# A scan and routed-experts layer on one core: the last weight set loaded behind the first row lists, and the second block's low part and turns moved

## What is computed

```python
xn = _layernorm(x, axis=-1)
x = x + _L0_attn_ref(xn, ...) + _L0_ffn_ref(xn, ...)
# attn: g, v, d = xn @ Wg + bg, xn @ Wv + bv, xn @ Wd + bd
#       h[t] = (0.001 + 0.998 * sigmoid(d)) * h[t-1] + sigmoid(g) * tanh(v)
# ffn:  scores = sigmoid(xf @ Wg.T + bg + bias); the two highest of 8 per token
#       out = gelu(xf @ Ws1.T + bs1) @ Ws2.T + bs2
#           + sum over the two of score * (gelu(xf @ W1[e].T + b1[e]) @ W2[e].T + b2[e])
```

## Time and profile before

| | us |
|---|---|
| median of 3 runs | 669.68 (669.53 to 670.26) |
| the profiled execution | 669.86 |
| its span, first to last instruction | 668.1 |
| PE busy | 640.3 (96%) |
| DVE busy | 535.2 (80%) |
| ACT busy | 407.1 (61%) |
| POOL busy | 277.1 (41%) |

### The profile page before, as it was taken

One profiled execution on the slowest core, in us unless ns is written; L12 is line 12 of the kernel. 1 busy time (PEld: TensorE's weight loads), 2 busy tenths in 40 slices (PEclk: granted clock), 3 DMA queues, 4 the chain that ended last, 5 costly groups with the idle time before them and its releaser, 6 DMA issues.

```text
span 668.1 us, 19052 instructions
## 1 busy us (share of the span) xinstructions
PE 640.3 (96%) x6168; PEld 506.0 (76%) x6168; DVE 535.2 (80%) x1431; ACT 407.1 (61%) x701; POOL 277.1 (41%) x262
## 2 busy tenths in 40 slices
PE   7989999999999998699999999999999999999994
PEld 6565756566665756588889988898889889898983
DVE  6988998999999889488887777677777767777774
ACT  6849696969687874264745454555555555555552
POOL 3043241324242541354545444435445555555423
PEclk9999999999999999799999999999999999999998
DMA  7324526171625242352424253545657576666732
GB/s 259 132 33 128 150 74 189 65 191 36 186 42 180 65 127 64 98 151 45 71 52 80 48 132 106 131 106 141 173 126 200 128 195 184 144 177 179 197 57 28
DMA packets 69472, 81.29 MB, mean 122 GB/s; under 512 B 25684, under 2 KB 61460, under 8 KB 66568
## 3 DMA queue, kind: packets, MB, share of 16 engines
q1 hardware_dynamic: 54264, 62.35, 30.8%
q0 software_dynamic: 15120, 17.77, 15.4%
HBM read 38.66 MB, written 18.10 MB: 85 GB/s over the span
## 4 chain that ended last, share of the span: by engine, by line
PE 80%; DVE 10%; issue 6%; ACT 2%; DMA 1%; another core or an unknown queue 0%; POOLq 0%; POOL 0%; DVEq 0%; ACTq 0%
PE bank L1340 31%; PE bank L1332 29%; PE bank L1320 6%; PE bank L1368 5%; PE bank L1391 4%; PE bank L1410 2%; DVE arena L953 2%; DVE arena L952 2%; DVE W L833 1%; PE bank L1311 1%; PE bank L1275 1%; DMA arena<-in_x 1%; DVE small L842 1%; ACT arena L644 1%; ACT W L612 1%
## 5 line engine op out<-in xcount | busy, mean ns | idle before, releaser
L1340 PE MATMUL bank<-W,arena 128*128 (+1 forms) x2112 | 278.5, 274 | 4.0 <-DVE arena L953 3.3
L1332 PE MATMUL bank<-rows,W 128*128 128x256 f16 (+1 forms) x1728 | 273.8, 296 | 3.4 <-issue 1.8
L655 ACT ACTIVATE arena<-bank,par 128x256 f32<-128x256 f32 (+2 forms) x344 | 166.8, 517 | 142.2 <-PE bank L1332 116.0
L1340 PEld LDWEIGHTS bank<-W,arena 128*128 128x128 f16 x2112 | 202.4, 98 | 40.6 <-issue 6.3
L1332 PEld LDWEIGHTS bank<-rows,W 128*128 (+1 forms) x1728 | 165.3, 98 | 57.2 <-issue 5.8
L576 POOL DMA_INDIRECT out<-arena,slot_adds x71 | 117.7, 1657 | 136.3 <-DVE arena L1217 71.8
L952 DVE TENSOR_SCALAR arena<-arena,par 128x256 f16<-128x256 f32 (+1 forms) x284 | 99.8, 351 | 55.8 <-ACT arena L655 36.5
L953 DVE SCALAR_TENSOR_TENSOR arena<-arena,par 128x256 f16<-128x256 f32 (+1 forms) x284 | 134.0, 472 | 10.1
L516 POOL DMA_INDIRECT lists<-entry,place x64 | 67.9, 1061 | 108.4 <-ACT arena L637 63.3
L1320 PE MATMUL bank<-rows,W 128*128 128x512 f16 x288 | 63.9, 379 | 0.1
L661 ACT ACTIVATE rows<-bank 128x1024 f16<-128x1024 f16 (+2 forms) x43 | 36.1, 839 | 43.8 <-PE bank L1410 31.1
(11 more groups left out here) (190 smaller groups left out, 546.3 us busy)
## 6 DMA issues: line engine op xcount, KB each, us to landing
stage<-in_w SPq DMA_DIRECT2D x36, 512.0 KB, 4.0
stage<-W SPq DMA_DIRECT2D x14, 1024.0 KB, 5.2
arena<-W SPq DMA_DIRECT2D x8, 1024.0 KB, 5.6
arena<-in_x SPq DMA_DIRECT2D x8, 512.0 KB
xhl_rows<-W SPq DMA_DIRECT2D x8, 512.0 KB
out<-arena SPq DMA_DIRECT2D x8, 512.0 KB
b2row<-in_b SPq DMA_DIRECT2D x22, 128.0 KB
arena<-in_b SPq DMA_DIRECT2D x21, 128.0 KB
```

The costliest lines, as they stand in the source:

```text
L655: ins = A(h32[k][:, c], ps_e[k][:, c], ACT.Gelu, bias=p[:, 4 + e * i + jj:5 + e * i + jj], scale=p[:, 0:1])
L1332: ins = T.matmul(bank_, weights(w, wp * HALF + c * H + j * P, P), rhs[:, 2 * xp + c, :], start=n == 0, stop=n == 3 * KD - 1)
L1340: ins = T.matmul(banks[t // 2][:, (t % 2) * D:(t % 2 + 1) * D], h[:, hp, t * P:(t + 1) * P], weights(w, (2 + wp) * HALF + j * D, D), start ...
```

## The change

Three things are moved; no instruction is added or removed, apart from where it stands.

1. SP: the four loads of set 8 leave the end of the loop over b and the end of slot 0's pass, and stand together behind the row list of slot 4, ahead of the values of slot 2.
2. End of sequence 0: DVE makes the second x's low part behind `split_wide(0, 5)`, the sixth split, instead of behind the eighth. PE turns high and low part one after the other behind the seventh `layer2`; before, the first turn stood there and the second behind the eighth.
3. Slots 4 to 7: DVE's `bias_rows` stands behind the seventh split instead of the sixth.

```diff
@@ SP, loop over b
-                if b:
+                if 0 < b < SEQS - 1:
                     for part in range(2):
                         next_weights(b + 1, 0, part)
@@ SP, loop over the slots
                 if n + 4 < SLOTS:
                     rows_list(s, order(n + 4))
+                if n == 0:
+                    for l in range(2):
+                        for part in range(2):
+                            next_weights(NW - 1, l, part)
                 if n + 2 < SLOTS:
                     values_of(s, order(n + 2))
...
                     adds_list(s, order(n + 2))
-                if n == 0:
-                    for part in range(2):
-                        next_weights(NW - 1, 1, part)
@@ DVE, opening
                 split_wide(0, 5)
+                x_low(1)
                 residual(0, 0, 1)
                 split_wide(0, 6)
                 split_wide(0, 7)
-                x_low(1)
                 low_turned(1, 1)
@@ DVE, slot
-                    if j == 5:
+                    if j == (6 if low is not None else 5):
                         bias_rows(s)
@@ PE, sequence
-                    if first and i >= 6:
-                        pe.wait_ge(*((xhi_ok, 2), (xhl_ok, 2))[i - 6])
-                        pe.wait_ge(*((r_ok, 2), (ev_act, RING + EVENTS))[i - 6])
-                        x_transposes(1, i - 6, (ps_t16, ps_low16[1])[i - 6])
+                    if first and i == 6:
+                        pe.wait_ge(xhl_ok, 2)
+                        pe.wait_ge(r_ok, 2)
+                        x_transposes(1, 0)
+                        pe.wait_ge(ev_act, RING + EVENTS)
+                        x_transposes(1, 1, ps_low16[1])
```

## The result

| | us |
|---|---|
| before, median of 4 runs | 669.66 (669.53 to 670.26) |
| changed kernel, median of 4 runs | 660.51 (660.00 to 661.39) |
| ratio | 0.9863, 95% interval 0.9846 to 0.9880 |
| its profiled execution, and the span | 661.39, 659.6 |

The change saves 9.15 us, 1.4%. That is less than the 1.4 us between the lowest and the highest of the four runs. The gain forecast against the medians, 8.2 us, lies inside the interval of the ratio (8.0 to 10.3 us), and between the two profiled executions the gain was 669.86 - 661.39 = 8.47, where 8.25 was forecast. So the question for the runs is where the other 0.7 to 0.9 us of the medians come from.

A forecast was written before the change was run, and what follows sets the result against it. PE was taken to set the pace, with its main hole at the hand-over to the slots. From 669.86, less 7.8 and 0.45, came 661.6, or 661.4 against the median; forecast 661.5, range 660.6 to 664.0 us.

The forecast's parts named there:

- Where the time lies: Hand-over from sequence 7 to slot 0: PE idles 6.27 us because SP waits to issue set 8's loads before the lists.
- The next thing late: Hand-over: with the gather's wait gone, DVE's eighth split, ending at 267.40, holds the last `layer2`.
- Size of part 1: Hand-over: moving the loads starts slot 0's second layer 7.8 us earlier, bounds 7.5 and 7.85.
- slack: Hand-over: gathered rows are there at about 264.2, PE wants them at 266.55, leaving 2.3 us.
- Part 2: End of sequence 0: moving low part and turns starts the logits earlier, gaining 0.45 us, bounds 0.3 and 0.5.
- the sum of PE's work: End of sequence 0: PE's gapless work from the seventh `layer2`, 43.87 to 47.55, takes 3.68 us in either order.
- the low part costs 0.33: End of sequence 0: the earlier low part delays later splits, so the seventh `layer2` starts at 44.2 instead of 43.87.
- Part 3: Slots 4 to 7: moving the bias rows costs 0, from 0.2 us gained to 0.3 lost.
- Loads behind the lists: Slots 0 and 1: the four loads, 2 MB, issued from 272.0 ahead of slot 2's values, cost nothing.
- The cover claimed: Slot 1: 10.5 us from the loads' issue to squaring the first part at 282.5, against landings of 4.2 to 7.3.
- The recorded estimate of 7.4 us: Slots 0 and 1: transfer time for 2.5 MB of loads and store at the skill's 341 GB/s.
- The range: Whole kernel: 660.6 to 664.0 us at 8 in 10, from term bounds 7.8 to 8.35, 0.4 scatter and most of one rival.

The follow-up runs named there:

- part 1 alone: Only the four loads of set 8 moved, against the kernel before: 656.12 against 663.88 us, ratio 0.9884.
- e7_one_ahead: Changed kernel with the first of the four loads left ahead of the row lists: 662.21 us against 664.10 for the kernel before, ratio 0.9969.
- e9_low_only: Kernel before with only DVE's low part moved behind the sixth split, PE's turns unmoved: 670.78 against 670.63 us, ratio 0.9997.
- e3_bias: Kernel before with only the bias rows of slots 4 to 7 moved: 664.12 us, ratio 1.0003.
- e6_no_bias: Changed kernel without the bias rows' move: 655.38 us against 664.10 for the kernel before, ratio 0.9871.
- e4_all: The whole changed kernel again, against the kernel before: 655.53 against 663.88 us, ratio 0.9872.
- e8_loads_late: Changed kernel with the four loads put behind slot 6's row list: 661.43 us against 664.10 for the kernel before, ratio 0.9956.
- e12_before_again: Kernel before, unchanged, traced again on the slower kind of chip: 669.95 us.
- e11_all_again: The whole changed kernel a third time, against the kernel before: 661.73 against 670.63 us, ratio 0.9867.
- e10_turns_only: Kernel before with only PE's turns moved behind the seventh `layer2`, low part unmoved: 670.41 against 670.63 us, ratio 1.0001.
- e5_before: Kernel before, unchanged, traced again on the faster kind of chip: 663.63 us.

## Why the prediction was off by a little: right in its mechanisms, short in its terms

**Where the time lies: right.** The hole at the hand-over was SP's queue, and it went away with part 1 alone (7.7 of 8.4 us). The next thing late was the eighth split, as named, and PE's wait for it 0.45 us.

**Size of part 1: the term that was mis-sized. It fits the execution that was read and is short for the median.** 7.85 was worked out and 7.8 taken; the two profiled executions give 7.76. But the hand-over of before was read from one execution, 14.11 us, and seven traces give 13.55 to 14.90 with a mean of 14.36. The kernels without a load ahead give 6.32 to 6.35. The mean gain is therefore 8.0, and single executions lie between 7.2 and 8.6. On the slower kind of chip, that of the comparison, the four traces have a mean of 14.53, so a gain of 8.2; on the faster kind three have 14.14, so 7.8. The forecast's bounds for this term, 7.5 to 7.85, described how DVE or PE would continue behind the hole and left out that the hole itself has a length that varies, with the landing of a small list behind big loads. The row for this was there (3.36 us for the list, a transfer of 2 KB) and was taken as a constant; without the loads it is 2.5. In the changed kernel that made no difference to PE, since there was slack (2.3 us by the forecast, 3.5 measured in e7_one_ahead), but it was the sign that the 14.38 us of POOL's wait held a DMA whose duration varies: 3.13 to 4.42 us with the two loads ahead of it.

**Part 2: right in mechanism, 0.1 to 0.15 us too small.** 0.45 forecast, 0.6 measured from the sixth `layer2`. What was mis-sized in it is the sum of PE's work, 3.68 us: it ran to the modelled end of the last turn, 47.55, while the next group starts some 0.15 us ahead of such an end. The step behind it, that the low part costs 0.33, was measured at 0.32 (e9_low_only). The measured 0.6 lies outside the term's bounds, 0.3 to 0.5.

**Part 3: right.** Nothing, by e3_bias and by e6_no_bias against e4_all.

**Loads behind the lists: right.** The cover claimed was 10.5 us against landings of up to 7.3; it was 10.6 against up to 9.2, and the first part, for which ACT would wait, landed 4.24 us after its issue in e8_loads_late. That run shows what lies past the cover. The Trainium skill ("DMA: Bandwidth & Descriptors", section "Issuing engines are not separate DMA queues") says that DMAs started by the scalar, sync or gpsimd engine run on the same 16 DMA engines and interleave; the landings of 9.2 us at most beside POOL's gathers and the store, against 7.3 at the opening, agree with it, but no run takes the gathers away. The recorded estimate of 7.4 us for the loads and the store is slightly low by its own figures: five transfers of 512 KB are 2.6 MB, which gives 7.7.

**The range: the step that failed.** Its low end was the upper bound of the terms, 8.35 us, and 0.4 us of scatter, which gives 660.9, and 0.3 us below that. The bound is what failed: part 1 gives 8.2 us on this kind of chip instead of at most 7.85, because the hole of before was taken from one execution, and part 2 gives 0.6 instead of at most 0.5. Together they are 8.8 us, a median near 660.9, which would still be in the range. The remaining 0.35 us of the gain of 9.15 is scatter, which was mis-sized as well. The 0.4 us came from three runs of before that lay within 0.7 us; on the chip of e9 to e12, 19 runs of the same kernel went from 668.78 to 674.07. Part of it is the stretch of the slots: in the trace of before short stalls could be read, for instance 0.68, 0.44 and 0.57 us ahead of 409.63, 456.40 and 458.65. I wrote only that PE's idle times are short, and not that they might vary, and the stretch differed by 1.8 us between executions on that kind of chip. How much of the 0.9 us between the gain of 9.15 and the 8.25 of the terms came from each is not settled. By the means of the traces the hole explains 0.4 and part 2 0.15, and the rest is within the scatter. That the median fell 0.1 us outside the range, and not inside, is chance: the 8.9 us of e11_all_again, taken from 669.66, would have given 660.8, just inside.

The same means give 8.8 us for the slower kind of chip, where both comparisons gave 8.9 to 9.2, and 7.8 + 0.6 = 8.4 for the faster kind, where they gave 8.4 to 8.7. This may be the difference between the kinds or not: the means are of four and three traces, and the intervals overlap.

## What to carry to other kernels

Where a queue's waiting instruction belongs to work that is needed late, look at what is written behind it: here two loads of 512 KB, wanted 29 us after their issue (261.48, 290.32), held four lists of 2 KB. Half of the cure is worth little: the first of the two loads, left ahead, still held the lists for 7 of the 10 us and gave back nearly four fifths of the gain. Then look how early the moved work must still be issued, because the four loads, issued 10.6 us further back, cost nearly as much. And a hole in one trace is one sample: before bounding what closing it gives, ask which DMA in it can vary, and let the range have that.

## What was not expected of the hardware

A list of 2 KB took 2.4 to 2.6 us from issue to the gather that waits for it with no load in front (six traces), 4.07 behind one of 512 KB (one trace), and 3.1 to 4.4 behind two (seven).

The granted clock fell to half in holes of 4.84 us (e7_one_ahead) and 4.01 us (e8_loads_late), as it had in the one of 6.27, and the work behind them began at half: up to 277 us in before, 274 in e7_one_ahead and 294 in e8_loads_late. In PE's waits of 1.67 us (e10_turns_only, up to 490.94) and 1.17 us (e11_all_again, up to 576.53) it stayed at 1.00.

The same kernel took 663.6 us on one kind of chip and 670 on another. Of these 6.3 us, by the traces of e5_before and e12_before_again, 4.5 lie in the slots from slot 4 on (331.38 against 326.85), 1.0 in slots 0 to 3 (46.44 against 45.44 up to the stalled group) and 1.25 in the hand-over, less 0.5 at the two ends of the kernel. About half of the 4.5 is short pauses of PE that the timeline lists; the rest is in no idle time that it lists.
